# Last self attention: VectorE copies the second transposed tile of a quad between the second and the third maximum

## The reference

```python
def _mha(q_in, kv_in, wq, bq, wk, bk, wv, bv, wo, bo):
    b = q_in.shape[0]
    q = (q_in @ wq.T + bq).reshape(b, -1, HEADS, HD).transpose(0, 2, 1, 3)
    k = (kv_in @ wk.T + bk).reshape(b, -1, HEADS, HD).transpose(0, 2, 1, 3)
    v = (kv_in @ wv.T + bv).reshape(b, -1, HEADS, HD).transpose(0, 2, 1, 3)
    scores = jnp.einsum('bhqd,bhkd->bhqk', q, k) * HD ** (-0.5)
    p = jax.nn.softmax(scores, axis=-1)
    o = jnp.einsum('bhqk,bhkd->bhqd', p, v)
    o = o.transpose(0, 2, 1, 3).reshape(b, -1, WIDTH)
    return o @ wo.T + bo
...
h = _layernorm(x, ln1_g, ln1_b)
x = x + _mha(h, h, sa_wq, sa_bq, sa_wk, sa_bk, sa_wv, sa_bv, sa_wo, sa_bo)
```

## Time and profile before

| what | value |
| --- | --- |
| median of 3 runs | 4731.24 us (4728.09 to 4732.82) |
| profiled execution, its own time | 4731.41 us |
| its span in the trace | 4729.6 us |
| TensorE busy | 3834.0 us (81% of the span) |
| VectorE busy | 3081.8 us (65%) |
| ScalarE busy | 2356.9 us (50%) |
| GpSimd busy | 2118.6 us (45%) |
| first maximum of the stages, at | 3909.59, 4114.75, 4321.30, 4525.79 us |

### The profile page before, as it was taken

One profiled execution on the slowest core, in us unless ns is written; L12 is line 12 of the kernel. 1 busy time (PEld: TensorE's weight loads), 2 busy tenths in 40 slices (PEclk: granted clock), 3 DMA queues, 4 the chain that ended last, 5 costly groups with the idle time before them and its releaser, 6 DMA issues. The chain is left out here.

```text
span 4729.6 us, 51833 instructions
## 1 busy us (share of the span) xinstructions
PE 3834.0 (81%) x16584; PEld 1973.5 (42%) x16584; DVE 3081.8 (65%) x4208; ACT 2356.9 (50%) x4461; POOL 2118.6 (45%) x2146
## 2 busy tenths in 40 slices
PE   6987898798789757887788878887788867877787
PEld 3443343344344324444444444444444434334343
DVE  2543263264235338999899998999899966464543
ACT  2321331232223147777677767777677635354352
POOL 0210020021002037888778877788777843132231
PEclk9998999899899979999999999999999989999998
DMA  3000000000000042322323333322323210000000
GB/s 137 1 1 11 0 1 5 7 1 1 11 0 1 5 130 84 90 76 74 88 81 84 90 95 85 90 74 76 88 81 83 70 73 2 11 1 11 1 5 5
DMA packets 132060, 215.92 MB, mean 46 GB/s; under 512 B 18960, under 2 KB 118544, under 8 KB 124496
## 3 DMA queue, kind: packets, MB, share of 16 engines
q1 hardware_dynamic: 131504, 201.08, 14.9%
q0 software_dynamic: 288, 11.53, 0.6%
HBM read 186.26 MB, written 26.30 MB: 45 GB/s over the span
## 5 line engine op out<-in xcount | busy, mean ns | idle before, releaser
L1758 POOL TENSOR_TENSOR m_db<-m_u,m_bb 128x512 f32<-128x512 f32 (+1 forms) x1280 | 1466.5, 1166 | 454.9 <-DVE m_hh L1710 452.2
L1710 DVE TENSOR_TENSOR_SCAN m_hh<-psum,m_kept,m_db 128x512 f32<-128x512 f32 (+1 forms) x1024 | 1194.8, 1200 | 30.3 <-POOL m_u L1803 17.5
L1509 ACT ACTIVATE psum<-m_dt,m_am 128x512 f32<-128x512 f32 (+1 forms) x1280 | 818.5, 644 | 414.5 <-DVE m_hh L1710 411.2
L1437 PE MATMUL psum<-cst,m_hh 128*128 128x128 f32 x4608 | 661.7, 284 | 333.0 <-DVE m_yt L1724 220.2
L1437 PEld LDWEIGHTS psum<-cst,m_hh 128*128 128x128 f32 x4608 | 521.9, 144 | 767.9 <-DVE m_yt L1724 433.1
L1447 PE MATMUL psum<-m_ys,cst 128*128 128x512 f32 x1024 | 544.6, 614 | 0.0
L797 POOL TENSOR_SCALAR a_pr<-a_pr,a_ri 128x512 f32<-128x512 f32 x256 | 174.5, 695 | 681.4 <-DVE a_ri L614 681.4
L1724 DVE SCALAR_TENSOR_TENSOR m_yt<-psum,m_bc,m_yt 128x512 f32<-128x512 f32 x600 | 436.2, 727 | 53.6 <-PE psum L1437 52.6
L1521 ACT ACTIVATE m_ys<-psum,m_bc 128x512 f32<-128x512 f32 x512 | 344.2, 672 | 26.7 <-PE psum L1437 25.8
L797 POOL TENSOR_SCALAR c_pr<-c_pr,c_ri 128x512 f32<-128x512 f32 x256 | 174.4, 695 | 407.1 <-DVE c_ri L733 403.1
L534 POOL TENSOR_TENSOR a_pr<-a_pr,a_ri 128x512 f32<-128x512 f32 x64 | 66.6, 1042 | 627.0 <-DVE a_ri L502 627.0
(11 more groups left out here) (222 smaller groups left out, 5809.6 us busy)
## 6 DMA issues: line engine op xcount, KB each, us to landing
m_bb<-b_rows SPq DMA_DIRECT2D x48, 1024.0 KB, 4.7
m_xr<-x_line SPq DMA_DIRECT2D x128, 192.0 KB, 3.8
m_bb<-b_rows SPq DMA_DIRECT2D x32, 768.0 KB, 4.3
m_xr<-x_line SPq DMA_DIRECT2D x128, 160.0 KB, 3.3
m_xr<-x_line SPq DMA_DIRECT2D x128, 128.0 KB, 3.1
m_xr<-x_line SPq DMA_DIRECT2D x128, 96.0 KB, 3.2
a_w1b<-w1b_in POOLq DMA_DIRECT2D x1, 7168.0 KB, 29.1
x_line<-m_xc SPq DMA_DIRECT2D x32, 192.0 KB, 4.6
```

The source lines that it names most:

```text
L1437: mm = nc.tensor.transpose(s[:, e * P:(e + 1) * P], hh[:, n % 2, e, t * P:(t + 1) * P], ident)
L1509: nc.scalar.activation(bank(DECAY[u % len(DECAY)])[:, 0:w], dt[:, g % 2, e, 0:w], ACT.Exp, scale=am[:, layer_of(g) % 2, e * DS + n:e * DS ...
L1710: nc.vector.tensor_tensor_scan(hh[:, n % 2, e, 0:w], bank(DECAY[u % len(DECAY)])[:, 0:w], db[:, u % 4, 0:w], kept[:, n, e:e + 1] if g % NI ...
L1758: nc.gpsimd.tensor_tensor(db[:, u % 4, 0:w], us[:, g % 2, e, 0:w], bb[:, at % 2, n % 4, 0:w], ALU.mult).then_inc(pool_done, pr.pool.step(f ...
```

## The change

In VectorE's loop the copy of the second transposed tile of the quad before (`empty(4 * i - 3)`) stood behind the four maxima of quad i. It now stands between the second and the third of them. Nothing else differs: the same instructions, the same waits, the same order on all other engines. As the copy carries the wait for its transposed tile, that wait moves with it, ahead of the third and the fourth maximum.

```diff
                     if i < plan.n:
-                        for u in range(4 * i, 4 * i + 4):
-                            maximum(u)
+                        maximum(4 * i)
+                        maximum(4 * i + 1)
                     if 1 <= i <= plan.n:
                         empty(4 * i - 3)
+                    if i < plan.n:
+                        maximum(4 * i + 2)
+                        maximum(4 * i + 3)
                     if i < plan.n:
                         inverse(2 * i)
```

## The result

| | before | changed |
| --- | --- | --- |
| median of the runs | 4731.24 us (5 runs, 4728.09 to 4734.33) | 4681.02 us (5 runs, 4674.1 to 4684.54) |
| profiled execution | 4731.41 | 4683.46 |
| its span | 4729.6 | 4681.7 |
| the 15 gaps between quads, four stages | 349.2 | 302.9 |

The ratio is 0.9895, with a 95% interval of 0.9881 to 0.9908. The change saves 50 us. The direction and the chain of waits were right, and one term of the sum, the clock, had the wrong sign.

A forecast was written before the change was run, and what follows sets the result against it. The prediction took a loop in which VectorE and TensorE wait for each other as the bound. 4731.4 - 43.0 (chain, four stages of 10.76) + 4 (clock) = 4692.4 us; own range 4687 to 4699, wider range 4682 to 4710.

The forecast's parts named there:

- the chain: In the four stages, the loop of maxima, copy, transposes, perhaps a product, and scores gets shorter: 43.0 us gained in all.
- The long loop: Step with the product with the values: from 6.79 to 5.59 us, gaining the whole 1.20; six per stage.
- the short one: Step without the product with the values: from 4.93 to 4.65 us, gaining 0.28; seven per stage.
- The gap with the output: Gap in which VectorE also takes out a sum: from 5.17 us to a short gap, gaining 0.52.
- The end of a stage: Step 16, without maxima: its first transposes wait for ScalarE's copy, 4.51 us instead of 5.59, gaining 1.08.
- what is late next: In short loops the third exponential's release holds the scores until 3.45 us; 0.93 of the 1.20 turns into waiting.
- the slack of the tile: VectorE's copy can start at 1.20 us and its tile can be taken at 0.98: 0.22 us of slack, no wait.
- the slower rival: The copy's tile comes later than 1.20 us, delaying two maxima, two exponentials and the next scores: 4744 us, chance 0.04.
- the clock term: TensorE's lower clock in the four stages: the loss of 10.6 us stays and 4 us come on top.
- the clock comes back: With fewer idle gaps, TensorE's slow stretches go away altogether: 4678 us, chance 0.07.

The follow-up runs named there:

- separate waits: Changed kernel, with each score product of a quad waiting for its own bank only: 4669.3 us beside 4730.6 of the kernel before, ratio 0.9876.
- copy first: Kernel before, with VectorE's copy moved behind the first maximum of the quad: 4699.8 us beside 4724.6, ratio 0.9944.
- long-only kernel: Kernel before, with the copy behind the second maximum only in odd steps from 3 on: 4694.5 us beside 4724.6, ratio 0.993.
- filler: Kernel before, with the transposes of each quad's third tile done twice: 4723.8 us beside 4724.6, ratio 0.9992; on another chip 4725.3 beside 4726.0, 0.9998.
- copy third: Kernel before, with the copy moved behind the third maximum in all steps: 4691.4 us beside 4724.6, ratio 0.9926.
- hybrid: Kernel before, with the copy behind the second maximum in odd steps from 3 on, behind the third in the others: 4674.6 us beside 4730.6, ratio 0.9883.
- both: Kernel before, with the copy placed as in the hybrid and each score product waiting for its own bank: 4665.8 us beside 4726.0, ratio 0.9877.

## Why the prediction was wrong

**Right: the chain.** The long loop was forecast at 5.59 and is 5.60, the short one at 4.65 and is 4.64 or 4.65. The gap with the output came down to a short one. The end of a stage was to gain 1.08 and gained 1.07. The chain's terms sum to 43.0 as forecast and to 38.8 + 4.3 = 43.1 by the gaps measured at full clock.

**Right: what is late next.** The scores wait 0.84 for the third exponential in each short loop (forecast 0.93). That is 38.7 - 12.2 = 26.5 us more than before, and I had said some 27. Most of the short loop's 1.20 went into that wait. The experiments with the copy behind the third maximum moved the short loop by 0.14, and separate waits by 0.13, each through that release alone.

**Right, but for one step: the slack of the tile.** 0.98 was forecast and 1.00 measured, in the kernel that wants it at 0.60. "The copy waits for nothing" holds in all steps but the first with a copy. There it waited 0.60 in stage 1 and 0.17 in stage 3, in a stretch of lower clock. That is the slower rival in small, and it is where nearly all of the remaining 2.5 us lie.

**Wrong: the clock term.** The prediction says "That loss stays, and a part comes on top", 10.6 us kept and 4 added. The kept loss had the right size before (10.0) but did not stay: 2.5 us were left of it. The term should have been -7.5 and was +4, so it was off by 11.5 us. The profiled execution (4683.5) lies 8.9 below the forecast: 11.5 less the 2.4 by which the parts between the stages grew and the 0.3 ahead of them. The median lies 11.4 below. I had reasoned that fewer idle gaps leave less room to hide slow matmuls. For a single stretch that is so: the one of 3.4 us that begins 3.8 us into stage 1 is in both traces, and in the second gap it cost 0.06 before (4.99 against 4.93) and 0.70 after (5.34 against the 4.64 of a short loop). But I had taken the number of stretches as given, without a reason. It fell from 13 to 4.

What the engine did before these falls, by the longest single idle of TensorE in a steady loop: 1.27 before (13 and 11 stretches in two traces), 1.51 with the copy first (9), 1.27 in the short loops of the long-only kernel (8), and 0.84 or less in all others: changed (4 and 4), filler (3 and 4; once a stage 1.04, at the output), copy third (3), hybrid (3), separate waits (4), both (4). The filler is the one that leaves the chain alone and only fills TensorE's idling, so for the stages the cause is shown and not only seen beside. It does two things at once, though: the pieces of idling get shorter and the work more. The pair of long loops only and copy third, with the same sum of idling and 8 against 3 stretches, speaks for the length of the pieces. But length alone does not order the counts either: 1.51 us went with 9, and 1.27 with 13, 11 and 8. The rule of the Trainium skill that the prediction had weighed (page "TensorE: Matmul & The Clock Gate", section "Part 1: The HAM clock gate (the "warmup" mystery)", activity releases the lower clock) agrees with the traces in the stages: 13 and 11 stretches before, 3 and 4 with the filler. Its rival, "the clock comes back" (4678, chance 0.07), was the nearest to the result, though one stretch a stage stayed. What I set against it, two stretches of one trace with 0.86 and 1.00, compared a part at the lower clock with one at the higher one. The first can be busier just because its matmuls are slower: 142 ns of busy time for each of its 138 against 105 for each of the 236. It could say nothing on the cause.

**Open.** In the whole kernel the filler brings nothing that can be measured, although its stages are 9 us shorter. So it is not shown that the 7.5 us are a net gain of the whole kernel. The record of the clock gives a hint. Inside the stages, their ends included, the lower clock took 48 and 41 us in the two traces of before and 14 in both of the changed kernel. Over the whole execution it took 533 and 513 us before and 519 and 533 after. Between and behind the stages it took 65 and 59 us before and 68 in both after, and these parts, whose instructions are the same, lasted 427.2 and 424.0 us before and 429.6 and 429.7 after. So part of the gain seems to be given back there. No experiment tests that. Two comparisons of before and changed gave 50 and 49 us, 6 to 7 more than the chain's 43, and that is the size of the term, but part of it may come from parts that no experiment touched, and with intervals of 43 to 56 and 41 to 55 us the chain's 43 alone is barely left out by the first and not by the second.

## What to carry to other kernels

When a wait that closes a loop is shortened, follow the loop with starts counted from one instruction. The gain is at most the smallest slack of the other releases into the same instruction, and it differs between iterations that carry other work. A loop in which TensorE idles, as it did here in pieces of 1.27 us, may also pay for a lower clock, and in the stages that part went with the idling, even where the work grew. Where a stretch of lower clock stays, a tighter chain pays more for it. A gain in the stages is not yet one of the whole kernel: the filler's was not. The four score products of 32 rows each took no longer here than one, so splitting their wait saved only what was ahead of the last one.

## What the runs showed of the hardware

- The same chain, at 4.93 and 6.79 a loop, lost 10 us of 349 to TensorE's lower clock with 1.27 us of idling in it, and 0.5 to 1.3 with 0.84 us and more work (all counted against 339.2).
- The step with VectorE's output lost most. In five of the eight stages in the two traces of before, the gap that follows was 8.4 us instead of 6.79. In the first stages the product behind it took 3.60 and 3.61 us instead of 1.93, behind an idle of 1.48 instead of 1.27. In the third stage of the first trace the same idle cost nothing. Second execution of before, TensorE:

```profile
3965.79 0.66 PE L690 MATMUL psum<-cst,c_pr 128*128 128x128 f32 x4 [1.48 <-DVE c_ptr L740]
3966.38 3.61 PE L705 MATMUL psum<-c_ptr,c_v3s 128*32 128x256 f32 x32
```

- With separate waits, the last score product on 32 rows took 1.16 us from its weights to the maximum that it releases. The four together, in the changed kernel, took 1.20 (4148.68 to 4149.88).
- The gaps of the four stages together repeat to 0.1 us from one execution to another (349.2 and 349.1; 302.9 and 302.8), while a single stage of before moved by 2.3 (85.4 and 87.7 in the third), and the part before the first stage by 8 us.
- All four stages of the changed kernel lose their 3.4 us at the lower clock at nearly the same place, 3.6 to 4.6 us into the stage, behind 3.05 us of idling.
